# Two dense attentions of a four-layer kernel: the negated row maxima are turned by VectorE in blocks of 32 and stored by four transfers, instead of one transpose on TensorE and one transfer

## The reference, cut to what matters

```python
attn = jnp.einsum('bnd,bmd->bnm', q * scale, k)
attn = (attn.reshape(B * nh, H, W, H, W) + rel_h[..., :, None] + rel_w[..., None, :]).reshape(B * nh, N, N)
attn = jax.nn.softmax(attn, axis=-1)
out = attn @ v
```

```python
attn = jnp.einsum('bhnd,bhmd->bhnm', q, k) * SCALE
attn = attn + jnp.einsum('bhnd,nmd->bhnm', q, r_p_k) * SCALE
attn = jax.nn.softmax(attn, axis=-1)
out = jnp.einsum('bhnm,bhmd->bhnd', attn, v)
```

## Time and profile before

| | |
|---|---|
| median of 3 runs | 7292.61 us (7291.99 to 7298.78) |
| the profiled execution, its own time | 7297.02 us |
| its span, first to last instruction | 7295.2 us |
| TensorE busy | 6065.1 us (83%) |
| VectorE busy | 3563.1 us (49%) |
| ScalarE busy | 2624.7 us (36%) |
| GpSimd busy | 2365.9 us (32%) |
| mean granted clock of TensorE | 0.891 |

### The profile page before, as it was taken

The page is one execution under the profiler, slowest core; times in us unless marked ns, Lnnn a source line. Parts: engine busy times, 40 slices in busy tenths (PEclk is TensorE's granted clock), DMA queues, the critical chain, the costliest instruction groups (busy, mean ns, idle before and its releaser), DMA issues. The chain is left out here.

```text
span 7295.2 us, 126941 instructions
## 1 busy us (share of the span) xinstructions
PE 6065.1 (83%) x42028; PEld 3280.5 (45%) x42028; DVE 3563.1 (49%) x5163; ACT 2624.7 (36%) x3475; POOL 2365.9 (32%) x2168
## 2 busy tenths in 40 slices
PE   5537999999986677666866797999999998879995
PEld 3425333333334233534756572333333333868885
DVE  2214666666644477444454534555555553451212
ACT  2212555555542211121322223555555554112221
POOL 0003555555530364211000014444444443033122
PEclk8758999999998788877875898999999998979997
DMA  2696333333332211100000154333333334747664
GB/s 89 95 158 190 86 89 89 89 89 89 90 66 74 89 58 43 42 0 1 1 1 0 46 177 113 98 101 99 98 98 101 99 98 141 238 176 240 219 228 158
DMA packets 1088658, 739.86 MB, mean 101 GB/s; under 512 B 800389, under 2 KB 971045, under 8 KB 1077702
## 3 DMA queue, kind: packets, MB, share of 16 engines
q1 hardware_dynamic: 1076038, 710.81, 35.7%
q0 software_dynamic: 12288, 25.18, 1.0%
HBM read 463.95 MB, written 278.00 MB: 102 GB/s over the span
## 5 line engine op out<-in xcount | busy, mean ns | idle before, releaser
L1080 DVE TENSOR_REDUCE L3B_nmax<-L3B_R 128x1 f32<-128x1024 f32 x768 | 939.3, 1224 | 678.2 <-PE L3B_R L953 658.5
L1080 DVE TENSOR_REDUCE L0B_nmax<-L0B_R 128x1 f32<-128x1024 f32 x768 | 939.3, 1224 | 466.0 <-PE L0B_R L953 452.5
L1067 ACT ACTIVATE L0B_PT<-L0B_R 128x1024 f32<-128x1024 f32 x768 | 785.4, 1023 | 603.4 <-PE L0B_R L963 566.2
L1067 ACT ACTIVATE L3B_PT<-L3B_R 128x1024 f32<-128x1024 f32 x768 | 785.2, 1023 | 603.3 <-PE L3B_R L963 560.6
L963 PE MATMUL L3B_R<-L3B_QS,L3B_KS 64*128 64x512 bf16 (+1 forms) x6144 | 795.4, 378 | 2.8 <-DVE L3B_nmax L1080 2.8
L963 PE MATMUL L0B_R<-L0B_QS,L0B_KS 64*128 64x512 bf16 (+1 forms) x6144 | 795.1, 378 | 2.8 <-DVE L0B_nmax L1080 2.8
L990 PE MATMUL L3B_O<-L3B_PT,L3B_VA 128*64 128x512 f32 x3072 | 743.7, 605 | 0.0
L963 PEld LDWEIGHTS L3B_R<-L3B_QS,L3B_KS 64*128 64x128 bf16 (+1 forms) x6144 | 267.6, 94 | 525.6 <-DVE L3B_nmax L1080 232.7
L963 PEld LDWEIGHTS L0B_R<-L0B_QS,L0B_KS 64*128 64x128 bf16 (+1 forms) x6144 | 259.8, 94 | 513.2 <-issue 239.8
L990 PE MATMUL L0B_O<-L0B_PT,L0B_VA 128*32 128x512 f32 x3072 | 409.1, 605 | 0.2 <-ACT L0B_PT L1067 0.2
L1395 POOL TENSOR_TENSOR L1B_qk<-L1B_Q,L1B_K 128x1536 f32<-128x1536 f32 x72 | 260.0, 3630 | 414.3 <-ACT L1B_V L1492 284.9
(11 more groups left out here) (410 smaller groups left out, 9266.2 us busy)
## 6 DMA issues: line engine op xcount, KB each, us to landing
L3F_weights<-in_L3F_w SPq DMA_DIRECT2D x79, 1251.0 KB, 5.8
scr_sumsL<-L3B_OT SPq DMA_DIRECT2D x96, 512.0 KB
L3C_sums<-scr_sumsL SPq DMA_DIRECT2D x96, 512.0 KB, 9.4
scr_rel<-L0R_terms SPq DMA_DIRECT2D x64, 384.0 KB
L0B_raw<-scr_rel SPq DMA_DIRECT2D x192, 128.0 KB
L3B_raw<-scr_rel SPq DMA_DIRECT2D x384, 64.0 KB
scr_flat<-flat_rows SPq DMA_DIRECT2D x48, 384.0 KB, 3.3
L0B_QS<-scr_parts SPq DMA_DIRECT2D x192, 96.0 KB, 2.1
```

The lines of the kernel that those rows point to most:

```text
L1067: nc.scalar.activation(PT[:, (8 * u + j) % NPT, :, :], score_pair(u, j), ACT.Exp).then_inc(s_exp, 1)
L1080: nc.vector.tensor_reduce(nmax[:, u % 2, t:t + 1], pair.rearrange("p j n -> p (j n)"), AX, ALU.max, negate=True).then_inc(s_mx, 1)
```

## The change

TensorE's transpose `max_rows` is gone, with its waits and the one in `pv`. `nmax` is widened to 32 columns per head, the unused ones set to zero once. VectorE transposes the whole 128 x 32 tile in square blocks of 32 into `NT`: block g of 32 partitions then holds, in its first 8 partitions, the maxima of queries 32g to 32g + 31 of each tile. It casts `NT` to bf16 in `MR`, now 128 x 32. Both happen after the `take_max` of step 1, the last of that head, instead of after that of step 2. SP stores the four blocks by one transfer each (8 partitions x 32 elements) and waits for all of them; the two loads of the row are as before.

```diff
-        nmax = st.sb("nmax", [P, 2, T])
+        nmax = st.sb("nmax", [P, 2, 32])
+        NT = st.sb("max_turned", [P, 32])
-        MR = st.sb("max_rows", [T, P], BF16)
+        MR = st.sb("max_rows", [P, 32], BF16)
...
-                sp.dma_start(scr["max"].rearrange("o (t n) -> (o t) n", t=T), MR[:, :]).then_inc(s_mo, 16)
-                sp.wait_ge(s_mo, 16 * (H + 1))
+                rows = scr["max"].rearrange("o (t g n) -> (o t) g n", t=T, g=4)
+                for g in range(4):
+                    sp.dma_start(rows[:, g, :], MR[32 * g:32 * g + T, :]).then_inc(s_mo, 16)
+                sp.wait_ge(s_mo, 64 * (H + 1))
...
-            def max_rows(H, u, bank):
-
-                pe.wait_ge(s_mx, T * (H + 1))
-                pos(pe, s_mc, H)
-                pe.sem_inc(s_pew, 1)
-                nc.tensor.transpose(O[0:T, bank, 0:P], nmax[:, u % 2, :], cst["ident"][:, :]).then_inc(s_mt, 1)
-
             def pv(H, u, b):
                 pe.wait_ge(s_exp, 8 * H + 2 * b + 2)
                 if b == 0:
                     pe.wait_ge(s_va, H + 1)
-                    if not isinstance(H, int) or H + 1 < HEADS:
-                        pe.wait_ge(s_mc, H + 2)
...
-                    if j == 2:
-                        nxt = ahead(H, u, i, 1)
-                        if nxt is not None:
-                            bank = u % 2 if L0 else 0
-                            if L0:
-                                pos(pe, s_on, H - 1)
-                            else:
-                                pos(pe, s_ot, 2 * H - 1)
-                            max_rows(nxt[0], nxt[1], bank)
...
-            def copy_rows(H, bank):
+            def copy_rows(H, u):
+                dve.wait_ge(s_mx, T * (H + 1))
+                nc.vector.transpose(NT[:, :], nmax[:, u % 2, :]).then_inc(s_mt, 1)
                 dve.wait_ge(s_mt, H + 1)
-                pos(dve, s_mo, 16 * H)
-                nc.vector.tensor_copy(MR[:, :], O[0:T, bank, 0:P]).then_inc(s_mc, 1)
+                pos(dve, s_mo, 64 * H)
+                nc.vector.tensor_copy(MR[:, :], NT[:, :]).then_inc(s_mc, 1)
+
+            nc.vector.memset(nmax[:, :, :], 0.0).then_inc(s_nz, 1)
+            dve.wait_ge(s_nz, 1)
...
-                    if j == 2:
+                    if j == 1:
                         nxt = ahead(H, u, i, 1)
                         if nxt is not None:
-                            copy_rows(nxt[0], u % 2 if L0 else 0)
+                            copy_rows(nxt[0], nxt[1])
```

More of the change, by code:

```diff
@@ L703, in attend @@
         s_passed = st.sem("pool_wait_passed")
+        s_nz = st.sem("max_set")
         s_mf = st.sem("max_scores_filled")
         s_mx = st.sem("max_taken")
-        s_mt = st.sem("max_transposed")
+        s_mt = st.sem("max_turned")
         s_mc = st.sem("max_copied")
@@ L1006, in _ @@
                 max_scores(R[:, 2 * p:2 * p + 2, :], n // T, n // T, n % T)
-                if n == T - 1:
-                    max_rows(0, 0, 0)
             pe.wait_ge(s_mx, 14)
```

## The result

The changed kernel takes 7258.55 us, the median of 5 runs (7252.31 to 7259.56). The kernel before takes 7298.78 us as the median of its 5 runs (7291.99 to 7303.18), the three that the prediction knew among them. The ratio is 0.9943, with a 95% interval of 0.9932 to 0.9954: about 40 us less. The profiled execution took 7258.55 us with a span of 7256.8, against 7297.02 and 7295.2: 38.4 us less in the span.

The account below looks back on a forecast made before the run. TensorE's own order was taken to bound both attentions (L0 and L3). The transpose's slot, -38.0 us, and start-up, +1.7, gave -36.3 us, so 7256.3 us from a median of 7292.61; range 7242 to 7267 us.

Parts of the forecast that it names:

- The slot of the transpose: TensorE, step 2 of each head in L0 and L3: removing the transpose saves 0.20 us, 2 x 95 times, 38.0 us less.
- TensorE's waits at nothing: TensorE's three waits and an increment before the transpose, and one wait at step 4's sums: removing them was priced at nothing.
- VectorE's part: VectorE after the reduction of step 1: block transpose and cast, 0.18 us each, about 0.5 us with two waits, hidden.
- The cover: Room before TensorE's scores of step 4 wait for VectorE's reduction of step 2: 1.6 us in L0, about 1.4 in L3.
- SP's part: SP's queue, each head: four stores of the maxima replace one, three more issues cost 1.2 us (0.8 to 1.4), hidden.
- The waits left: SP's wait for the row of maxima would still be there, at 1.2 to 1.7 us per head.
- The start-up, +1.7 us: Start of each stage, where SP's order binds: +1.2 us in L3, +0.5 in L0, with bounds 0 and 3.
- The sum: Whole kernel: -38.0 + 1.7 = -36.3 us, from a median of 7292.61 to 7256.3 us; chance 0.80.
- a gain of the whole 273 ns: Rival, TensorE: each transpose gives back its full duration, 51.9 us, 50.2 with the start-up, 7242.4 us; chance 0.08.
- SP and VectorE as the bound: Two rivals: SP's four transfers don't overlap, 7454 us, chance 0.04; VectorE late for step 4's scores, 7446 us, chance 0.02.
- no change: Rival: the slot closes up elsewhere, another engine sets the pace, heads stay at 15.15 and 17.76 us, 7293 to 7294; chance 0.06.

## Why the prediction was right

**The slot of the transpose, -38.0 us.** Right in mechanism and size. The distances from sums to scores are those foretold (1.00 and 1.87 us; 0.99 and 1.87 found), heads in L0 fell to 14.95 us. Putting the instruction back took all of the gain away, and putting its waits back took none.

**TensorE's waits at nothing.** Right there, and shown for all but the one in `pv`. But it is no rule for this engine's waits: two others, behind the wait that ends last, cost 0.16 us a head. The prediction had "the sequencer was ahead" for its reason, and that is the condition.

**VectorE's part.** The transpose was taken at 0.18 us and takes 0.21, the cast 0.18 as taken, the pair about 0.5 us as taken (1494.64 to 1495.16). The cover was reckoned at 1.6 us in L0 and is 1.6; ten transposes crossed it at the place named.

**SP's part.** Three more issues were taken at 1.2 us and cost 1.0 (3 x 0.34), inside 0.8 to 1.4. The loads of the row, reckoned at 3.06 us after the sums of step 2 began, start at 2.91 (before, 3.18). The waits left were put at 1.2 to 1.7 us per head and are 1.5 and 1.8. The rule of the Trainium skill against splitting ("DMA: Bandwidth & Descriptors", Rules for kernel authors), read as a full landing for each part, isn't borne out for four parts of 8 x 64 bytes: the loads of the row come 1.23 us after the last of the four was issued (1496.42 to 1497.65), as they came 1.25 after the single one before. What was missed is that SP's idle time is a mean. It hides the turn of SP's loop, 2.7 us at one head in 12 in L0 and at one in 6 in L3, in the kernel before too, and the spare that counts is what is left to make that up. With four stores it is enough, with eight it isn't.

**The start-up, +1.7 us.** This term was wrong, in sign too. Measured up to the second sums of head 0, by which TensorE has passed one of the 190 transposes, L0 took 29.79 us from its first maximum tile (678.83 to 708.62), against 29.59 (679.83 to 709.42), so +0.4 net of that one's 0.20. That is as taken, and TensorE does stall where it was foretold, ahead of the first maximum tile of head 2 (the row names ScalarE, as the earlier trace rows does; before, the tile came 1.06 us after its scores, without a stall). It comes 2.30 us after SP issued the last transfer of that placing, at 699.95; in L3 before it was 2.33 (4449.25 to 4451.58).

```profile
702.25 0.39 PE L957 MATMUL L0B_R<-L0B_KS,L0B_QS 64*128 64x512 bf16 x2 [0.49 <-ACT L0B_PT L1051]
```

In L3, from the first reduction to the same sums, it was 34.52 us (4425.83 to 4460.35) and is 32.47 (4406.93 to 4439.40), -1.85 net of the slot, where +1.2 had been taken. In sum -1.45, 3.2 us from the prediction's term and outside its bounds of 0 and 3. The prediction took the 1.91 us of idle time in the earlier trace rows for SP's order plus a landing, and as given. But it came from one slow landing. In the trace of before, the store of key parts ahead of it was issued at 4443.38 and the next placing at 4447.02, 3.6 us later; in the changed kernel, from 4425.02 to 4426.87, it is 1.85. SP's waits in the kernel before name the landing of these parts, with 3.1 us at the longest; in L0 of both kernels and in L3 of the changed one the longest is 1.2 or 1.3.

```profile
SPq L802 <- DMA scr_parts<-L3B_kq_parts: 5.5, 3, 3.1
```

What made the one slow isn't shown, so nothing says that it would have come again. The idle time had a price of its own, too, which the prediction didn't see. This is the window behind it in the kernel before, with the columns of the earlier trace rows:

```profile
4452.70:4456.10 3.40, 3.40 (x20) 1.05 (x16) 2.00 (x4) 1.51 (x2) 0.00 (x0) 0.50 0.46 128
```

The granted clock is 0.50 there, its lower level of 1.2 GHz; eight matmuls of scores take 1.92 us (from 4453.66) instead of the 1.04 of the earlier trace rows. About half of the 3.4 us, 1.7, is lost by it. In the changed kernel the granted clock is 1.00 from 4434 to 4438 us, so both the stall and this loss are gone. In its place stands another stall:

```profile
4430.91 0.21 DVE L1069 STREAM_TRANSPOSE L3B_max_turned<-L3B_nmax 128x32 f32<-128x32 f32 x1
4431.16 1.51 DVE L1072 CAST L3B_max_rows<-L3B_max_turned 128x32 bf16<-128x32 f32 x1
...
4433.86 1.04 PE L967 MATMUL L3B_R<-L3B_QS,L3B_KS 64*128 64x512 bf16 x8 [1.03 <-DVE L3B_nmax L1064]
```

```profile
4430.51 2.12 POOL L922 TENSOR_TENSOR L3B_QS<-L3B_raw,L3B_QS 128x1024 bf16<-128x1024 f32 x1 [0.18 <-POOL L3B_QS L921]
```

The cast ends at 4432.67, GpSimd's instruction at 4432.63, and the late reduction holds TensorE for 1.03 us. That is a cost of the change that the prediction didn't see, since it priced the cast by its length alone.

**The sum.** -38.0 - 1.45 = -39.5 us for the two stages, where 40.0 is found; the span fell by 38.4, the prediction said 36.3. From the median of five runs of before, 7298.78, the predicted step would give 7262.5, and 7258.55 was measured; the predicted 7256.3 rested on the first three runs, whose median lay 6.2 us lower. So the base was 6.2 us low and the step 3.9 us too small, and the two offset each other: part of the nearness is luck. The rivals: a gain of the whole 273 ns is excluded in the profile by the starts, and by the 38.6 us that the transpose put back costs in the two stages; SP and VectorE as the bound were each brought about by more of the same work, and had room at the change's own size; no change is excluded by the interval.

## What to carry to other kernels

On an engine that sets the pace, an instruction is worth its slot between the starts of its neighbours, not its duration: here 0.20 us and not 0.273, 190 times. Before moving its work elsewhere, compare what the other engine adds with its cover in the tightest head, the loop's turn included, not with its mean idle time. And put waits that are long fulfilled ahead of the one that ends last: that was worth 28 us in the two stages, where the whole change brought 40. And measure the stages that an edit touches: 38 and 52 us could be told apart in them, and not in the time of the whole kernel.

## What the runs showed of the hardware that was not expected

- A VectorE cast from SBUF to SBUF is held while a GpSimd instruction runs: 0.16 to 0.18 us alone, up to 2.09 us held. The cast out of PSUM in the kernel before was 269 to 280 ns in all 192 heads; most of them met GpSimd's work only in passing, but the one of 4435.53 lay wholly inside a GpSimd cast of 1.04 us (from 4435.11) and took 278 ns. So moving a small operation's source from PSUM to SBUF can make its duration uncertain, at no cost here outside the start.
- Two waits against register values cost TensorE 0.16 us a head when they stand behind the wait that ends last, and nothing measurable ahead of it.
- SP loses about 2.7 us where its loop turns (3.34 against 0.69 us between the same two transfers). What the time goes into isn't shown.
- Behind some idle times of TensorE, 1.91 us at the start of L3 before and 2.67 us with eight stores, the granted clock fell to 0.50 for a time, a loss of about 1.7 us on top of the idle time; behind another of 2.37 us it stayed at 1.00. What tells them apart was not looked for.
- Transposes that are each awaited follow one another at 0.25 us, for 211 ns of duration; small stores issued back to back at 0.34 us, for 0.29.
